# Two batches' first layers side by side in the head of a two-layer transformer on one core

## The reference

```python
h = _layernorm(x, axis=-1) * (1 + ca) + sa
...
# layer 0, attention: 16 heads of 16 features, softmax within blocks of 64 tokens
attn = softmax(einsum('bhnld,bhnmd->bhnlm', qb, kb), axis=-1)
...
# layer 0, coupling cycles: three times
for _ in range(NUM_CYCLES):
    tf = _coupling_net(out, ...)          # 256 -> 256 -> 128 -> 64 -> 1, gelu, sigmoid
    combined = 0.7 * gf + 0.3 * tf
    coupling = BASE_COUPLING + adaptive_range * (combined - 0.5) * 2.0
    out = out + coupling * _twist(out)
...
# layer 1, attention: 8 heads of 64 features, causal, over 512 tokens
term1 = where(causal_mask, 0.0, qc_s @ vu^T)
lookahead = where(causal_mask, sigmoid(qu_s @ ku^T), 0.0)
Su = einsum('bhij,bhkj->bhik', term1, lookahead)
scores = qc_s @ kc^T - silu(Su)           # causal softmax, then times vc
...
# layer 1, experts: each of 8 experts takes its best 128 of 512 tokens
g, m = top_k(probs.transpose(0, 2, 1), k)
h = gelu(einsum('nekd,edf->nekf', xin, w1)); h = einsum('nekf,efd->nekd', h, w2)
out = zeros.at[batch_idx, m].add(g[..., None] * h)
```

## Time and profile before

| | us |
|---|---|
| median of 3 runs | 2082.56 |
| lowest and highest | 2076.69, 2085.29 |
| the profiled execution, own time | 2077.9 |
| its span in the profile | 2076.5 |
| PE busy | 1971.1 |
| DVE, ACT, POOL busy | 1111.0, 947.1, 685.9 |
| mean granted clock of TensorE | 0.977 |

### The profile page before, as it was taken

One profiled execution on the slowest core, in us unless ns is written; L12 is line 12 of the kernel. 1 busy time (PEld: TensorE's weight loads), 2 busy tenths in 40 slices (PEclk: granted clock), 3 DMA queues, 4 the chain that ended last, 5 costly groups with the idle time before them and its releaser, 6 DMA issues.

```text
span 2076.5 us, 30527 instructions
## 1 busy us (share of the span) xinstructions
PE 1971.1 (95%) x11224; PEld 1321.3 (64%) x11224; DVE 1111.0 (54%) x2912; ACT 947.1 (46%) x2046; POOL 685.9 (33%) x818
## 2 busy tenths in 40 slices
PE   6669999999999999999999999988999999999998
PEld 4436556655755665575566557544666678888887
DVE  5355485566558556655855665596433437323221
ACT  2326565465556546555654655553454521111111
POOL 2103343334234332423333342333334323333332
PEclk9779999999999999999999999999999999999999
DMA  3020000001000000100000010005102033333333
GB/s 106 0 94 1 1 16 22 21 1 36 11 11 13 25 21 1 37 11 11 12 26 22 1 37 11 11 1 171 30 21 57 17 94 74 77 76 79 74 79 66
DMA packets 59560, 76.67 MB, mean 37 GB/s; under 512 B 7107, under 2 KB 52686, under 8 KB 59158
## 3 DMA queue, kind: packets, MB, share of 16 engines
q1 hardware_dynamic: 46310, 57.15, 8.3%
q0 software_dynamic: 12288, 16.79, 4.8%
q10 hardware_dynamic: 816, 0.79, 0.1%
HBM read 53.58 MB, written 21.00 MB: 36 GB/s over the span
## 4 chain that ended last, share of the span: by engine, by line
PE 84%; DVE 11%; ACT 2%; issue 2%; DMA 1%; POOL 1%; SPq 0%; DVEq 0%; ACTq 0%; POOLq 0%
PE bank L812 12%; PE bank L1025 10%; PE bank L1038 10%; PE bank L875 6%; PE bank L911 3%; PE bank L930 3%; PE bank L899 3%; PE bank L826 3%; PE bank L638 3%; PE bank L943 3%; PE bank L797 3%; PE bank L884 3%; PE bank L664 2%; PE bank L862 2%; PE bank L706 2%; PE bank L673 2%
## 5 line engine op out<-in xcount | busy, mean ns | idle before, releaser
L812 PE MATMUL bank<-hT,wqkv 128*128 128x512 f32 x640 | 302.3, 605 | 2.9 <-DVE th L1551 1.8
L1025 PE MATMUL bank<-xin,ew 128*128 128x256 f32 x1024 | 239.6, 386 | 1.3 <-issue 1.3
L1260 ACT ACTIVATE h<-bank 128x512 f32<-128x512 f32 x128 | 76.5, 597 | 346.0 <-PE bank L1025 345.7
L1802 POOL TENSOR_TENSOR s<-s,ri 128x256 f32<-128x256 f32 (+3 forms) x128 | 160.6, 1272 | 212.7 <-DVE ri L1573 212.5
L1038 PE MATMUL bank<-ew,h 128*128 128x256 f32 x1024 | 229.5, 382 | 1.0 <-ACT h L1260 1.0
L1038 PEld LDWEIGHTS bank<-ew,h 128*128 128x128 f32 x1024 | 195.2, 191 | 31.8 <-issue 3.9
L1025 PEld LDWEIGHTS bank<-xin,ew 128*128 128x128 f32 x1024 | 191.0, 192 | 31.5 <-issue 8.0
L1236 ACT ACTIVATE s<-s,mn 128x128 f32<-128x128 f32 (+3 forms) x256 | 141.1, 552 | 135.4 <-DVE mn L1566 135.4
L812 PEld LDWEIGHTS bank<-hT,wqkv 128*128 128x128 f32 x640 | 115.8, 192 | 127.9 <-issue 123.9
L1840 POOL DMA_INDIRECT out<-y,indices x64 | 102.8, 1606 | 284.6 <-DVE y L1709 199.5
L1709 DVE SCALAR_TENSOR_TENSOR y<-bank,gates,gbe 128x256 f32<-128x256 f32 x64 | 30.9, 484 | 254.9 <-PE bank L1038 254.8
(11 more groups left out here) (246 smaller groups left out, 3524.7 us busy)
## 6 DMA issues: line engine op xcount, KB each, us to landing
ew<-L_ffn_w SPq DMA_DIRECT2D x24, 1024.0 KB, 8.4
x<-L_attn_x SPq DMA_DIRECT2D x8, 512.0 KB, 4.0
x_scratch<-x SPq DMA_DIRECT2D x8, 512.0 KB, 2.9
x1s<-x_scratch SPq DMA_DIRECT2D x8, 512.0 KB, 5.7
out<-x1s SPq DMA_DIRECT2D x8, 512.0 KB, 2.9
xn_scratch<-n_xn SPq DMA_DIRECT2D x8, 512.0 KB, 2.9
wqkv<-w_qkv SPq DMA_DIRECT2D x1, 3072.0 KB, 10.0
wqkv<-L_wmod SPq DMA_DIRECT2D x2, 1024.0 KB, 8.1
```

The lines of the kernel that those rows point to most:

```text
L812: mm = te.matmul(banks[i][:, :], b1.wqkv[:, kk, j * CH1 + hp * P:j * CH1 + (hp + 1) * P], b1.hT[:, kk, :], start=(kk == 0), stop=(kk == KC ...
L1025: mm = te.matmul(banks[i][:, f * 2 * P:(f + 1) * 2 * P], w1[:, kk, (2 * n + f) * P:(2 * n + f + 1) * P], xin[:, kk, :, :].rearrange("p h s ...
L1802: done = g.tensor_tensor(sc, sc, b1.ri[u % 2][:, m, :].unsqueeze(2).to_broadcast([P, 2, w]), ALU.mult)
```

## The change

Batch 1's first layer no longer stands in the first period but beside batch 0's, in front of all periods. For this it has buffers of its own: a class `First` holds the buffers and semaphores of a first layer, and there are two states, "a" for batches 0 and 2 to 7, and "b" for batch 1 alone. State b lies in memory that the second layer's attention and tail use later. The layer's result `b1.hT` exists twice and alternates by batch. In the periods "+" now means b+2 instead of b+1, the order within the table is another, and there are six periods, for b = 0 to 5. The head, and everything from attention 6 on, are written out in two tables, HEAD and LAST, in which an item starts with its batch; `experts*3` stands for the next three steps of the experts' sequence, `choice0` and `choice1` for the next step of `top`, `rank`, `pos` of a group. Attention 6 has no first layer beside it; tail 5 and `choice0` stand there. The POOL engine now clears v and k of both states at the step `x0` of batch 0, which in HEAD stands behind `stats` of batch 0. In the six engine functions each buffer `b0.x` of the first layer becomes `f.x`, with `f = k.first[state_of(b)]`, and each count by batch becomes one by lap; no instruction of the computation is added or taken out. Clearing of two pieces of `b1.w` moves from `setup0` to the first `w`.

```diff
+HEAD = """
+    0silu:0 0wqkv_load:0 0stats:0 0mod_load:0 0x0:0 1stats:0 0cols:0 0setup:0 0norm:0 0mod_load:1 1x0:0 0cols:1
+    0w0_load:0 0rows:0 0feat:0 0kq:0 1norm:0 1mod_load:0 0kq:1 1mod_load:1 1feat:0 0setup0:0 0sc0:0 0sc0:1
+    0ga0_load:0 0wt0:0 1silu:0 1kq:0 0wt0:1 1kq:1 0sc0:2 0v:0 0sc0:3 0tp0:0 0tp0:1 1sc0:0 1ga0_load:0 0wt0:2 0wt0:3
+    0v:1 1wt0:0 1v:0 1sc0:1 0sc0:4 1wt0:1 0tp0:2 0pv0:0 1tp0:0 0wt0:4 0tp0:3 1sc0:2 1sc0:3 1tp0:1 1wt0:2 1wt0:3 1v:1
+    0pv0:1 0sc0:5 1sc0:4 1tp0:2 0wt0:5 1tp0:3 1pv0:0 1wt0:4 0tp0:4 0sc0:6 0sc0:7 0wt0:6 0wt0:7 0tp0:5 1pv0:1 1tp0:4
+    1sc0:5 1cols:0 0w1_load:0 0tp0:6 0pv0:2 1wt0:5 0tp0:7 1sc0:6 1tp0:5 1wt0:6 0pv0:3 1sc0:7 1pv0:2 1wt0:7 0out0:0
+    0out0:1 1tp0:6 0stats:1 0norm:1 1tp0:7 1pv0:3 1out0:0 0feat:1 1out0:1 1stats:1 0cn1:0 0gc:0 0cn2:0 0twist:0
+    1norm:1 0gc:1 0cn3:0 0gc:2 0cn4:0 1feat:1 0cn1:1 1cols:1 0cn2:1 1cn1:0 1rows:0 0tables:0 0cn3:1 1gc:0 0cn4:1
+    1cn2:0 1gc:1 1twist:0 1cn3:0 1gc:2 1cn4:0 0cn1:2 1cn1:1 0cn2:2 1cn2:1 1cn3:1 0cn3:2 1cn4:1 0cn4:2 1cn1:2 1cn2:2
+    0gate0:0 1cn3:2 1cn4:2 1gate0:0 0fin0:0 1fin0:0 0stats:2 1stats:2 0norm:2 1norm:2 0feat:2 1feat:2
+"""

 PERIOD = """
-    proj:0.0 proj:0.2 +x0:0 -x1_load:0 -attend:10 -weigh:11 proj:0.3 +stats:0 +norm:0 +ga0_load:0 turn_vu:0 proj:0.1
-    +feat:0 look:0.0 term:0 look:0.1 look:0.2 look:0.3 +kq:0 +kq:1 proj:1.3 -turn:11 +sc0:0 +sc0:1 +v:0 +wt0:0
-    +wt0:1 -attend:11 w:0.0 w:0.1 +v:1 +tp0:0 +tp0:1 +sc0:2 +sc0:3 +wt0:2 +pv0:0 vc:0 proj:0.4 +wt0:3 +sc0:4 +tp0:2
...
+    -x1_load:0 proj:0.0 +x0:0 +stats:0 proj:0.1 +norm:0 proj:0.3 +ga0_load:0 proj:0.2 proj:0.4 -weigh:11 +feat:0
+    look:0.0 term:0 look:0.1 look:0.2 -attend:10 -turn:11 +kq:0 +kq:1 turn_vu:0 -attend:11 vc:0 +sc0:0 +wt0:0 +sc0:1
+    look:0.3 +sc0:2 vc:1 +tp0:0 w:0.0 +v:0 +v:1 +wt0:1 +wt0:2 +tp0:1 +sc0:3 -o_out:3 +tp0:2 +wt0:3 proj:1.2 +sc0:4
...
+    su:6 +cn2:2 turn:5 sw:6 -probs:0 +cn3:2 attend:5 o_out:1 sc:6 weigh:6 su:7 w:2.1 sw:7 +cn4:2 proj:3.0 proj:3.1
 """

+LAST = """
+    6proj:0.0 5weigh:11 6proj:0.2 6proj:0.3 6proj:0.4 6turn_vu:0 6proj:0.1 5attend:10 5turn:11 6look:0.0 6term:0
+    5x1_load:0 6look:0.1 5attend:11 6vc:0 6vc:1 6look:0.2 5o_out:3 6look:0.3 6w:0.0 6vc:2 6su:0 5out1:0 6sw:0 6sc:0
+    6weigh:0 6w:0.1 6proj:1.2 5out1:1 5stats_t:0 6su:1 6sw:1 5norm_t:0 6proj:1.1 6vc:3 6proj:1.0 6turn:0 5feat_t:0
+    6look:1.0 6sc:1 6weigh:1 6look:1.1 6look:1.2 6attend:0 6turn_vu:1 6proj:1.3 6turn:1 6su:2 6sw:2 6sc:2 6look:1.3
+    6term:1 5gate:0 6proj:1.4 6proj:2.3 5softmax:0 5probs:0 6proj:2.1 6weigh:2 6proj:2.0 6w:1.0 choice0 6w:1.1
+    6attend:1 6su:3 6sw:3 6turn:2 6su:4 6sw:4 6sc:3 6sc:4 6look:2.0 choice0 6su:5 6weigh:3 6proj:2.2 6attend:2
+    choice0 6sw:5 6look:2.1 6o_out:0 6weigh:4 6turn_vu:2 6proj:2.4 6turn:3 6look:2.2 choice0 6sc:5 6term:2 choice0
+    6look:2.3 6w:2.0 6attend:3 6weigh:5 6proj:3.2 choice0 6turn:4 choice0 6su:6 6su:7 6sw:6 6sw:7 6sc:6 6attend:4
+    6w:2.1 6turn_vu:3 6proj:3.3 6su:8 choice0 6sw:8 6proj:3.0 6weigh:6 6turn:5 6proj:3.1 6attend:5 6o_out:1
+    6look:3.0 6look:3.1 choice0 6sc:7 6term:3 6look:3.2 choice0 6look:3.3 choice0 6sc:8 6weigh:7 6turn:6 6proj:3.4
+    7proj:0.0 6su:9 choice0 6weigh:8 6w:3.0 6attend:6 6turn:7 6sw:9 6w:3.1 choice0 6attend:7 6turn:8 6su:10 6sw:10
+    6sc:9 choice0 6sc:10 6attend:8 choice0 6weigh:9 7proj:0.3 6o_out:2 6su:11 6sw:11 7proj:0.4 7proj:0.2 6turn:9
+    6weigh:10 6sc:11 choice0 6attend:9 7proj:0.1 6weigh:11 7turn_vu:0 6turn:10 choice0 7look:0.0 7look:0.1 7look:0.2
+    7look:0.3 7term:0 experts 6attend:10 7w:0.0 choice0 6turn:11 7proj:1.2 7w:0.1 6attend:11 6x1_load:0 6o_out:3
+    7proj:1.0 experts 7su:0 experts*3 6out1:0 experts 7sw:0 experts*2 7sc:0 7weigh:0 6out1:1 7vc:0 experts 7vc:1
+    7proj:1.1 7vc:2 7turn:0 experts 7su:1 7sw:1 7sc:1 7look:1.0 experts 7proj:1.3 6stats_t:0 7vc:3 experts 7su:2
+    7attend:0 7sw:2 7look:1.1 7proj:1.4 experts 7look:1.2 7look:1.3 experts 6norm_t:0 7sc:2 7term:1 7weigh:1
+    7turn_vu:1 experts*5 6feat_t:0 experts*2 7turn:1 experts*2 7w:1.0 7attend:1 experts 7su:3 experts 7proj:2.0
+    7sw:3 experts 7su:4 7weigh:2 7w:1.1 7sw:4 7sc:3 7sc:4 experts*2 7turn:2 experts*3 7proj:2.1 7proj:2.2 experts*2
...
+    experts 7turn_vu:3 experts 7su:8 7look:3.0 7sw:8 experts 7sc:7 experts*5 7look:3.1 7sc:8 7term:3 7look:3.2
+    experts*3 7look:3.3 7weigh:7 7attend:6 7w:3.0 experts 7proj:3.4 7weigh:8 7su:9 7turn:7 experts*3 7w:3.1
...
+    7su:11 experts 7turn:9 7sw:11 7sc:11 7attend:9 7x1_load:0 7turn:10 7weigh:11 experts*3 7attend:10 experts*6
+    7turn:11 experts 7attend:11 7o_out:3 experts*3 7out1:0 7out1:1 experts 7stats_t:0 experts*3 7norm_t:0 experts*7
+    7feat_t:0 experts*2 7gate:0 experts*2 7softmax:0 experts*3 7probs:0 choice1 experts*3 choice1 experts*4 choice1
+    experts choice1 choice1 choice1 experts*2 choice1 choice1 experts*2 choice1 experts*7 choice1 choice1 choice1
+    experts choice1 choice1 choice1 experts*2 choice1 choice1 experts*12 choice1
+"""

+def written(table):
+    for item in table.split():
+        step, place = item.split(":")
+        yield step[1:], int(step[0]), place_of(place)
 
 def period(b):
     for item in PERIOD.split():
         step, place = item.lstrip("+-").split(":")
-        batch = b + {"+": 1, "-": -1}.get(item[0], 0)
+        batch = b + {"+": 2, "-": -1}.get(item[0], 0)
...
 def all_steps():
...
+    order = list(written(HEAD))
     for b in range(B - 2):
         order += period(b)
-    order += with_choice(list(period(B - 2)), [x for chunk in choose_chunks(0) for x in chunk])
-    beside_last = 6
-    chunks = [c for m in range(beside_last) for c in experts_chunks(m)]
-    interleave(order, attention_chunks(B - 1), (iter([[]] * 4 + chunks), 4 + len(chunks), 1.0),
-               (late(6, tail_chunks(B - 2)), 6 + NTAIL, 0.6))
...
+    experts = chain.from_iterable(experts_steps(m) for m in range(NUNIT))
+    choice = [choose_steps(group) for group in range(2)]
+    for item in LAST.split():
+        if item.startswith("experts"):
+            order += islice(experts, int(item[8:] or 1))
+        elif item.startswith("choice"):
+            order.append(next(choice[int(item[6:])]))
+        else:
+            order += written(item)
+    order += experts
     return order

+class First:
+    def __init__(self, nc, name, x, ga, norm, hT, early, sb):
+        self.x, self.ga, self.norm, self.hT = x, ga, norm, hT
+        self.tmp = norm.xn[:, 0:2, :]
+        self.k = early(f"k0{name}", [P, KC, NBLK, NR, LB])
+        self.v = early(f"v0{name}", [P, NBLK, NR, 64])
+        self.q = sb(f"q0{name}", [P, KC, NBLK, 2, LB])
...
+        self.sem = {n: nc.alloc_semaphore(n + name) for n in FIRST_SEMAPHORES}
...
-        self.hT = sb("hT1", [P, KC, T])
+        self.hT = [sb("hT1", [P, KC, T])]
...
+def state_of(b):
+    return 1 if b == 1 else 0
+
+def lap_of(b):
+    return b - 1 if b > 1 else 0
...
+        self.first = [First(nc, "a", x, ga, norm, hT, low, low),
+                      First(nc, "b", b1.x, b1.ga, b1.norm, b1.hTt, Arena(nc, b1.early_at, b1.late_at),
+                            Arena(nc, b1.late_at, middle))]
+        b1.hT.append(low("hT1b", [P, KC, T]))
...
     for step, b, n in k.order:
         if step == "x0" and b == 0:
-            g.memset(b0.v[:, :, :, :], 0.0)
-            g.memset(b0.k[:, :, :, :, :], 0.0).then_inc(s["setup_pool"], 1)
+            for state in k.first:
+                g.memset(state.v[:, :, :, :], 0.0)
+                g.memset(state.k[:, :, :, :, :], 0.0).then_inc(s["setup_pool"], 1)
```

533 lines of the change are left out of this document (204 added, 329 removed).

## The result

The changed kernel takes 2006.47 us (median of 4 runs, 2003.81 to 2008.09), the kernel before 2083.81 beside it on the same chip: a ratio of 0.9634, 95% interval 0.9609 to 0.9659. Forecast were 2034, with a range of 2010 to 2062. The profiled execution took 2008.09 us, its span is 2006.5.

What follows compares the result with a forecast made beforehand. The prediction took PE to bound the kernel nearly everywhere, so only idle time and low clock could be won. Head +25, period 6 -65 and attention 7 -5 gave -45 on 2077.9: 2033, plus 1 for the median: 2034, range 2010 to 2062.

Steps and rivals of the forecast that it cites:

- The head, +25: Before the first projection: batch 1's first layer beside batch 0's lengthens it from 145 to 170 us, +25.
- Full clock in the head: Before the first projection: the filled head would run at full granted clock throughout, a rival's case; the sum kept part of the loss.
- The rule about shared interfaces: VectorE instructions with two SBUF inputs contend with GpSimd; priced against the head, at most 8 us longer there.
- Period 6, -65: Attention 6 with tail 5, one first layer fewer: 204.5 to 140 us, 10 us of it lost, -65.
- The wait on the ranks: Attention 6: PE's 4.7 us wait loses its cause through room on DVE and 16 steps between rank and pos.
- Attention 7 beside the experts, -5: Last attention in written order, six units beside it: half its losses won back, -5 us, bounds -15 and +5.
- The periods, 0 with bounds of 8: New order in six periods: 1.9 us to win in each and as much to lose; 0, bounds -8 and +8.
- Full clock and good cover: Faster rival: head 158, attention 6 loses 4, attention 7 gives 10 back; -68 us, 2010; chance 0.12.
- Attention 6 starves: Rival: without filler attention 6 loses 35 us instead of 10 and attention 7 wins nothing; 2063; chance 0.18.

Runs made afterwards that it cites:

- old_period: The changed kernel with the period table of the kernel before, its "+" items now meaning b+2; 1996.04 us, ratio 0.9593.
- old_seven: The changed kernel with attention 7, experts, tails and second top-k ordered by the rules of the kernel before, attention 6 as written; 2043.2 us, ratio 0.9825.
- no_mix: The changed kernel with the 15 items of batch 7 and the experts ahead of attention 6's last o_out moved behind it; 2018.79 us, ratio 0.9703.
- close_ranks: The changed kernel with 2 instead of 12 expert steps between the second rank and its pos; 2014.98 us, ratio 0.9673.
- filled_seven: old_seven with nine more expert steps in the end of attention 7 and the second pos 12 steps behind its rank; 2035.89 us, ratio 0.9774.
- before_spread: The kernel before with 8 of 18 first top-k steps left in period 6 and 10 moved into the start of attention 7; 2069.4 us, ratio 0.9944.
- bare_end: The changed kernel with the 11 expert steps between the last two o_out of attention 7 moved behind it; 2015.54 us, ratio 0.9681.
- bunched: The changed kernel with the 18 steps of the first top-k set behind every second step near the end of attention 6; 2018.7 us, ratio 0.9699.
- serial head: The changed kernel with batch 1's first-layer steps behind all of batch 0's in the head; 2101.48 us, ratio 1.0101.

## Why the prediction was right, and where it was wrong

**The head, +25: right, +27.7.** The stages came close to their forecasts: first scores 36.4 (38), `cn1` of batch 0 at 99.2 (95), the last cycle of batch 1 starts on DVE at 158.2 (157). DVE is busy for 122.8 us of it (124), PE for 140.2 at a mean clock of 0.90 (116 at full clock). The new head is bound by the two chains in turn, as the longest waits of PE in it show: for the normalised input, for a gelu in batch 1's last cycle and for the result of that cycle. The 5.5 us for a load are at the start of the program.

```profile
PE bank L551 <- DVE n_xn L1219: 6.7, 2, 4.6
PE bank L520 <- DMA wqkv<-L_wmod: 5.5, 1, 5.5
PE bank L687 <- ACT a1b L1096: 4.5, 1, 4.5
PE bank L717 <- DVE hT1t L1445: 3.3, 1, 3.3
```

**Full clock in the head: it did not come.** The granted clock is 1.00, 1.00, 0.90, 0.86 and 0.50 in the five stages. Where the second batch fills PE (45.0 of 45.7 us busy) it is 1.00 where one batch alone had 0.75; in the last stage, where both batches wait for DVE and PE works 7.7 of 15.6 us, it is as low as before. The Trainium skill's statement in "TensorE: Matmul & The Clock Gate", section "What's actually happening", that the default is throttled and activity releases it, agrees with both. The rival that I drew from it, a head at full clock throughout, took the whole head for filled.

**The rule about shared interfaces: right about the place.** L1419 takes 688 ns in the new head, as its twin did before, and 1148 ns in the new period against 986. L1427 shows it best: 1095 ns as a mean where POOL works beside it, 678 where it doesn't (old_period). This agrees with "GPSIMD Engine Reference" of the Trainium skill, section "Specifications", which has VectorE instructions with two SBUF inputs contend with GpSimd. I weighed that rule against the head, where it changed nothing, and not against the new table of the period, where the durations changed.

**Period 6, -65: right for the wrong kernel.** old_seven shows this part without the seam: 204.5 to 138.6 us, -65.9. The filler that was gone was not missed inside the attention. At its end it was, and old_seven, which has the bare end, shows 7.8 us of idle in the 138.6, near the 10 of the forecast. But the forecast was for the changed kernel, of which it said in half a sentence that the projections of batch 7 lie beside the end of attention 6. There that loss is gone, and the cover, with the distance of the first ranks, is worth 13.8 us (no_mix). The agreement with old_seven is luck: the term kept a loss that its own argument took away.

**The wait on the ranks: one of two reasons.** I gave room on DVE and distance in the list in one breath, and the distance as 16 steps; it is 9 for the first group and 13 for the second. The room alone does not do it. DVE has the same room in old_seven, and PE still waits 4.2 us there, since `pos` follows `rank` at once. The distance does, as close_ranks (6.3 us) and filled_seven (3.8 us gone) show for the second group. Nor is the distance enough as a count of steps: before_spread has 2 and no wait, since full projections stand in them.

**Attention 7 beside the experts, -5: the step that failed.** I wrote: "I take half back in idle and clock, less some new stalls". The part measured -39.3 us, the last stretch of the changed kernel less that of old_seven. 13.8 of them belong to the seam, so that -25.5 stand against the -5, outside its bounds of -15 and +5. Of the 35 us by which the last stretch beat the forecast, this term has 20, the seam 14, attention 6 itself 1. Three things were wrong with the term. The lost time was counted as idle time only, 17 us by rows 3 and 9, and a microsecond of PE idle costs more than itself. By the single edits it costs 1.4 (close_ranks) to 1.7 (bare_end), with no_mix, bunched and filled_seven in between, and over the whole of old_seven 39.3 us for 22.8 of idle. Next, I took the share that can be won from no row at all, though the periods showed in rows 3 that this kernel's written orders lose 1% where its rules lose 4; the likeliest value was nearly all, not half. Last, I said that six units lie beside attention 7 as before. The table has seven, with four `hidden` products in its bare end where the old rule has one (bare_end). Of these, the first is a size that the trace of before could have given: from 1418.6 to 1432.5 PE had no idle at all and a clock of 0.81. I read that row as one without loss. It stands behind the wait of 4.7 us on the ranks, and 13.9 us at 0.81 are 2.6 us lost, so the wait cost 7.3, or 1.6 times its length (an estimate from these rows). The 17 us priced so are 27.

**The periods, 0 with bounds of 8: inside, but not nothing.** The new order costs 7.6 us in this pair of executions and 10 in the medians (old_period). "There are 1.9 us to win in each and as much to lose" was the right size; the step did not look for collisions, which are the likely source of the sign.

**The rivals.** "Full clock and good cover", 2010, is nearest in time, and only half of it came: the good cover of attention 6 did, but it had the head at 158 (it was 172.7) and attention 7 at -10. "Attention 6 starves" fell: old_seven has 7.8 us of idle there, not 35. The serial head is real (2101) but is not what the change does.
